# Attention sums of a graph network: one-hot matrices made on ScalarE, all weight products on VectorE, rings of eight

## The reference, cut to what matters

```
a = jnp.exp(a - amax[edge_dst])
a = a / (jax.ops.segment_sum(a, edge_dst, num_segments=n)[edge_dst] + 1e-12)
ns = jax.ops.segment_sum(vs * a[..., None], edge_dst, num_segments=n)...
nv = jax.ops.segment_sum(vv * a[..., None, None], edge_dst, num_segments=n)...
```

## Time and profile before

| | |
|---|---|
| runs | 12,377.51 us median (12,340.81 to 12,393.03) |
| span of the profiled execution | 13,633.7 us |
| first run of `attention_sums` | 3,190 to 3,757 us of the span |
| second run | 10,572 to 11,134 us |
| busy over the span | PE 70%, DVE 63%, POOL 59%, ACT 32% |

### The profile page before, as it was taken

How to read it: one execution, slowest core, us unless ns; L and a number is a source line. 1 busy time by engine, 2 the same in 40 slices (tenths; PEclk the granted TensorE clock), 3 DMA queues, 4 the chain that set the end, 5 groups by cost and what they waited for, 6 DMA issues and landing times. The chain is left out here.

```text
span 13633.7 us, 220854 instructions
## 1 busy us (share of the span) xinstructions
PE 9563.9 (70%) x44805; PEld 7451.6 (55%) x44805; DVE 8593.3 (63%) x21214; ACT 4334.4 (32%) x10856; POOL 8081.0 (59%) x8212
## 2 busy tenths in 40 slices
PE   2998989863656666666655777777775657888885
PEld 2888888853544222222244666666664545555554
DVE  4677777778734555555534777777777765555553
ACT  1444444430022222222212555555554002222221
POOL 4777777755624888888822555555552643555550
PEclk7777777777956777777765888888887987888885
DMA  3444444435602888888852222222221652222221
GB/s 93 105 107 103 107 102 107 105 100 158 188 20 50 132 132 132 131 132 131 132 148 85 68 69 68 68 69 69 68 69 49 183 134 57 71 71 70 73 72 46
DMA packets 1350634, 1320.06 MB, mean 97 GB/s; under 512 B 508622, under 2 KB 1147330, under 8 KB 1349894
## 3 DMA queue, kind: packets, MB, share of 16 engines
q0 software_dynamic: 347904, 594.12, 23.6%
q1 hardware_dynamic: 854716, 713.61, 18.2%
q10 hardware_dynamic: 147914, 11.21, 0.8%
HBM read 800.64 MB, written 517.55 MB: 97 GB/s over the span
## 5 line engine op out<-in xcount | busy, mean ns | idle before, releaser
L737 POOL DMA_INDIRECT e_gs<-tab_src,e_ix x1568 | 1685.9, 1075 | 1253.8 <-DVE e_msg L2066 785.5
L737 POOL DMA_INDIRECT e_gd<-tab_dst,e_ix x1568 | 1670.5, 1065 | 478.0 <-issue 473.4
L676 PE MATMUL e_psF<-w_ident,e_F 128*128 128x128 f32 x6272 | 1394.2, 335 | 727.6 <-ACT e_F L1954 495.6
L788 PE MATMUL e_psS<-e_rows,e_same 128*128 128x480 f32 x1568 | 1113.4, 876 | 857.7 <-DVE e_same L762 857.7
L1772 POOL DMA_INDIRECT e_g<-tab_src,e_er x976 | 977.0, 1001 | 852.0 <-DMA e_er<-edge_rows 600.8
L676 PEld LDWEIGHTS e_psF<-w_ident,e_F 128*128 128x128 f32 x6272 | 951.5, 180 | 895.9 <-issue 844.5
L806 POOL DMA_INDIRECT acc<-e_sums,e_row x784 | 1248.6, 1593 | 239.0 <-issue 220.5
L706 ACT ACTIVATE e_FT<-e_psF 128x384 f32<-128x384 f32 (+1 forms) x2352 | 1069.7, 455 | 941.7 <-PE e_psF L676 587.3
L788 PEld LDWEIGHTS e_psS<-e_rows,e_same 128*128 128x128 f32 x1568 | 431.4, 293 | 1549.4 <-issue 1522.2
L1563 PE MATMUL s_psS<-s_wv,s_hot 128*128 128x168 f32 (+1 forms) x3904 | 714.2, 331 | 596.0 <-POOL s_wv L1521 574.8
L712 ACT ACTIVATE e_O<-e_psO 128x352 f32<-128x352 f32 (+1 forms) x1568 | 689.7, 440 | 995.6 <-remote 434.0
(11 more groups left out here) (492 smaller groups left out, 25450.2 us busy)
## 6 DMA issues: line engine op xcount, KB each, us to landing
s_val<-val SPq DMA_DIRECT2D x488, 320.0 KB
val<-e_O SPq DMA_DIRECT2D x392, 320.0 KB
acc<-w_zeros SPq DMA_DIRECT2D x392, 139.5 KB
n_ag<-acc SPq DMA_DIRECT2D x56, 960.0 KB
e_krow<-in_src_t SPq DMA_DIRECT2D x196, 256.0 KB
sums<-e_total SPq DMA_DIRECT2D x244, 192.0 KB
e_es<-in_es SPq DMA_DIRECT2D x196, 130.0 KB
e_gs<-tab_src,e_ix POOLq DMA_INDIRECT x1568
```

The costliest lines, as they stand in the source:

```text
L676: last = nc.tensor.transpose(psF[:, P * g:P * g + P], F[:, k, P * g:P * g + P], ident[:, :])
L737: pool.indirect_dma_start(into[t][u][:, k, :], None, tables[t], bass.IndirectOffsetOnAxis(ix[u][:, t, k:k + 1], 0))\
L788: nc.tensor.matmul(psS[(k) % len(psS)], T["same"][u][:, k, :], values[:, k, :], start=True, stop=True)\
```

## The change

POOL keeps the shift, now in place in `key`, and copies the result into a float tile `rel` (a new instruction, with a wait between them), two steps behind the load; it also keeps the copy of the weights. ACT makes the one-hot matrices: four `Abs` activations of 128 columns each, |lane - rel|, with `rel` as per-partition bias, three steps behind the load, and one `Relu` of 1 - x over all 512 columns, a step later. DVE takes all weight products, one of 256 columns and three of 128. `val`, `pb`, `key` and `total` become rings of eight, the other buffers stay at four; the two semaphores `weighted_s` and `weighted_v` become `weighted` (DVE) and `copied` (POOL), and `key` gets a semaphore of its own. SP waits for one of them only. The hardware loop now holds eight steps.

```diff
-        RING = 4
+        RING, HALF = 8, 4
...
-        SUM, TOTAL, STORE, LAST = 1, 3, 7, 7
+        REL, APART, HOT, WEIGH, SUM, TOTAL, STORE, LAST = 2, 3, 4, 4, 5, 7, 10, 10
...
         def _(sp):
...
                 if m := i_of(0):
                     i, u, j = m
-                    wait_apart(sp, sem("weighted_s"), i - RING + 1, sem("sp_passed"))
-                    wait_apart(sp, sem("weighted_v"), i - RING + 1, sem("sp_passed"))
+                    wait_apart(sp, sem("weighted"), i - RING + 1, sem("sp_passed"))
...
         def _(pool):
...
-                    tt(rel[u][:, :], key[u][:, :], W["shift"][:, bass.ds(i, 1)].to_broadcast([P, TM]), ALU.add).then_inc(sem("rel"), 1)
-                    wait_apart(pool, sem("summed"), i - RING + 1, sem("pool_passed"))
-                    for d in range(2):
-                        weigh(tt, u, C0 + C1 * d, C1)
+                if m := i_of(REL):
+                    i, u, j = m
+                    wait_apart(pool, sem(f"key{u}"), (j + 1) * 16, sem("pool_passed"))
+                    wait_apart(pool, sem("apart"), i - HALF + 1, sem("pool_passed"))
+                    nc.gpsimd.tensor_tensor(key[u][:, :], key[u][:, :], W["shift"][:, bass.ds(i, 1)].to_broadcast([P, TM]), ALU.add)\
+                        .then_inc(sem("shifted"), 1)
+                    wait_apart(pool, sem("shifted"), i + 1, sem("pool_passed"))
+                    nc.gpsimd.tensor_copy(rel[u % HALF][:, :], key[u][:, :]).then_inc(sem("rel"), 1)
+                if m := i_of(WEIGH):
+                    i, u, j = m
+                    wait_apart(pool, sem(f"in{u}"), (j + 1) * 32, sem("pool_passed"))
+                    wait_apart(pool, sem("summed"), i - HALF + 1, sem("pool_passed"))
+                    nc.gpsimd.tensor_copy(wv[u % HALF][:, :, CX:width], pb[u][:, :, :]).then_inc(sem("copied"), 1)
...
         def _(dve):
...
-                    weigh(tt, u, 0, C0)
-                    weigh(tt, u, C0 + 2 * C1, C1).then_inc(sem("weighted_s"), 1)
-                    dve.wait_ge(sem("rel"), i + 1)
-                    tt(hot[u][:, :, :], bcast(W["lane"][:, :], 1, TM), bcast(rel[u][:, :], 2, P), ALU.is_equal).then_inc(sem("hot"), 1)
+                    tt(scalars(wv[u % HALF]), scalars(val[u]), bcast(pb[u][:, :, :], 3, C0 // H), ALU.mult)
+                    for d in range(3):
+                        part = lambda t: t[:, :, C0 + C1 * d:C0 + C1 * d + C1].rearrange("p t (h c) -> p t h c", h=H)
+                        last = tt(part(wv[u % HALF]), part(val[u]), bcast(pb[u][:, :, :], 3, C1 // H), ALU.mult)
+                    last.then_inc(sem("weighted"), 1)
...
         def _(act):
...
+                if m := i_of(APART):
+                    i, u, j = m
+                    act.wait_ge(sem("rel"), i + 1)
+                    wait(act, sem("summed"), i - HALF + 1)
+                    for k in range(TM):
+                        last = nc.scalar.activation(hot[u % HALF][:, k, :], W["lane"][:, :], ACT.Abs, bias=rel[u % HALF][:, k:k + 1], scale=-1.0)
+                    last.then_inc(sem("apart"), 1)
+                if m := i_of(HOT):
+                    i, u, j = m
+                    act.wait_ge(sem("apart"), i + 1)
+                    nc.scalar.activation(hot[u % HALF][:, :, :], hot[u % HALF][:, :, :], ACT.Relu, bias=1.0, scale=-1.0).then_inc(sem("hot"), 1)
```

More of the change, by code:

```diff
@@ L1472, in attention_sums @@
         ring = lambda name, shape, n, dt=F32: [S.sb(f"{name}{u}", shape, dt) for u in range(n)]
-        RING = 4
+        RING, HALF = 8, 4
         val, pb, key = ring("val", [P, TM, CX], RING), ring("pb", [P, TM, H], RING), ring("key", [P, TM], RING, I32)
-        rel, hot, wv = ring("rel", [P, TM], RING, I32), ring("hot", [P, TM, P], RING), ring("wv", [P, TM, width], RING)
+        rel, hot, wv = ring("rel", [P, TM], HALF), ring("hot", [P, TM, P], HALF), ring("wv", [P, TM, width], HALF)
         total = ring("total", [P, width], RING)
-        psS = [S.ps(f"psS{u}", [P, 512]) for u in range(RING)]
+        psS = [S.ps(f"psS{u}", [P, 512]) for u in range(HALF)]
         values, weights = blocks_of(D["val"]), blocks_of(D["probs"][H])
         targets = D["dst_sorted"].rearrange("p t -> (p t)").rearrange("(m q k) -> m q k", q=P, k=TM)
-        SUM, TOTAL, STORE, LAST = 1, 3, 7, 7
+        REL, APART, HOT, WEIGH, SUM, TOTAL, STORE, LAST = 2, 3, 4, 4, 5, 7, 10, 10
         block = ctx.enter_context(nc.Block())
-        def weigh(tt, u, a, n):
-            heads = lambda t: t[u][:, :, a:a + n].rearrange("p t (h c) -> p t h c", h=H)
-            return tt(heads(wv), heads(val), bcast(pb[u][:, :, :], 3, n // H), ALU.mult)
         @block.sync
@@ L1505, in _ @@
             for u in range(RING):
[L1506 removed]
+                sp.wait_ge(sem(f"stored{u}"), 16 * -(-(V - u) // RING))
         @block.gpsimd
         def _(pool):
[L1510 removed]
             def body(i_of):
[L1513 removed]
+                if m := i_of(REL):
                     i, u, j = m
[L1515 to L1521 removed]
+                    wait_apart(pool, sem(f"key{u}"), (j + 1) * 16, sem("pool_passed"))
[9 more added lines that the diff above has]
+                    nc.gpsimd.tensor_copy(wv[u % HALF][:, :, CX:width], pb[u][:, :, :]).then_inc(sem("copied"), 1)
             steps(pool, V, LAST, body, RING)
@@ L1530, in body @@
             def body(i_of):
-                if m := i_of(0):
+                if m := i_of(WEIGH):
                     i, u, j = m
-                    dve.wait_ge(sem(f"in{u}"), (j + 1) * 48)
-                    wait(dve, sem("summed"), i - RING + 1)
-                    weigh(tt, u, 0, C0)
-                    weigh(tt, u, C0 + 2 * C1, C1).then_inc(sem("weighted_s"), 1)
-                    dve.wait_ge(sem("rel"), i + 1)
-                    tt(hot[u][:, :, :], bcast(W["lane"][:, :], 1, TM), bcast(rel[u][:, :], 2, P), ALU.is_equal).then_inc(sem("hot"), 1)
+                    dve.wait_ge(sem(f"in{u}"), (j + 1) * 32)
+                    wait(dve, sem("summed"), i - HALF + 1)
+                    scalars = lambda t: t[:, :, 0:C0].rearrange("p t (h c) -> p t h c", h=H)
+                    tt(scalars(wv[u % HALF]), scalars(val[u]), bcast(pb[u][:, :, :], 3, C0 // H), ALU.mult)
[3 more added lines that the diff above has]
+                    last.then_inc(sem("weighted"), 1)
                 if m := i_of(TOTAL):
@@ L1545, in body @@
                     nc.vector.scalar_tensor_tensor(out=total[u][:, :], in0=total[(u - 1) % RING][:, :], scalar=W["keep"][:, bass.ds(i, 1)],
-                                                   in1=psS[u][:, 0:width], op0=ALU.mult, op1=ALU.add).then_inc(sem("totals"), 1)
+                                                   in1=psS[u % HALF][:, 0:width], op0=ALU.mult, op1=ALU.add).then_inc(sem("totals"), 1)
             dve.wait_ge(sem("empty"), 1)
@@ L1557, in body @@
                     i, u, j = m
-                    wait_apart(pe, sem("weighted_v"), i + 1, passed)
+                    wait_apart(pe, sem("copied"), i + 1, passed)
                     wait_apart(pe, sem("hot"), i + 1, passed)
-                    wait_apart(pe, sem("weighted_s"), i + 1, passed)
-                    wait_apart(pe, sem("totals"), i - RING + 1, passed)
+                    wait_apart(pe, sem("weighted"), i + 1, passed)
+                    wait_apart(pe, sem("totals"), i - HALF + 1, passed)
                     for k in range(TM):
-                        last = nc.tensor.matmul(psS[u][:, 0:width], hot[u][:, k, :], wv[u][:, k, :], start=(k == 0), stop=(k == TM - 1))
+                        last = nc.tensor.matmul(psS[u % HALF][:, 0:width], hot[u % HALF][:, k, :], wv[u % HALF][:, k, :],
+                                                start=(k == 0), stop=(k == TM - 1))
                     last.then_inc(sem("summed"), 1)
```

12 lines of the change are left out of this document (3 added, 9 removed).

## The result

Nineteen runs of the changed kernel have a median of 12,392.61 us (12,360.45 to 12,430.79), nineteen of the kernel before, beside them, 12,362.84 us (12,326.02 to 12,393.03). The ratio is 1.0028, 95% interval [1.0018, 1.0038]: slower by 0.28%, 30 us by the medians and 35 by the ratio. That is less than the 0.5% up to which the prediction spoke of no change, but nineteen runs of each tell it from zero, and the forecast was 10 us to the other side. One run of `rings_only` (19,271 us) and one of `cut_after` (21,517 us), both kernels of the experiments, fell into a slow state and are left out of the ratios.

What follows compares the result with a forecast made beforehand. SP's queue was taken as the bound, ACT's queue afterwards: 488 x 0.09 + 8 = +52 us in the profiled execution, turned into about -10 us for the runs, 12,365 us; range 12,250 to 12,600.

Steps and rivals of the forecast that it cites:

- The bound: Attention-sums function: SP's queue never stops and fills the step of 2.31 us; no engine or load bandwidth does.
- Deeper rings for nothing: Loads in the function: slots of the four-deep rings were already free, so deeper rings and earlier loads gain nothing.
- DVE, POOL and ACT's engine: Engine work per step: DVE 1.99 to 1.69 us, POOL 1.7 at most, ACT 1.8; none becomes the bound.
- ACT's queue becomes the bound: ACT's queue in the function: 2.0 + 0.43 - 0.04 = 2.39 us a step, 0.09 us above before.
- Fill and drain: Ends of each function run: three steps deeper, 4 us a run, 8 us in all.
- From the profile to the runs: Runs 9.2% below the span: perhaps stretched queue instructions; between a 20 us gain and 52 loss, about -10 us.
- +52: Sum in the profiled execution: 488 x 0.09 + 8 us on 13,633.7 us, +0.4%.
- Nothing outside these stretches is edited, so only what changes in a step counts: Stages outside the attention-sums function: no effect counted; only the time of its 488 steps was priced.
- A: Rival, faster: in real runs DVE, not the queues, bounds the function; step 1.85 us, gain 98 us, 12,280 us; chance 0.24.
- B: Rival, slower: ACT's queue costs more, at 0.8 us added a step of 2.75 us, 220 us, 12,600 us; chance 0.15.
- C: Rival, much slower: ACT's register reads or DMA issues wait for its empty engine; 3.8 us a step, 13,110 us; chance 0.08.
- D: Rival: `Abs` and `Relu` lie in different tables, two table loads a step, +1,252 us; chance 0.03.

Runs made afterwards that it cites:

- rings_only: Kernel before with the deeper rings, longer loop and earlier loads alone, work split as before: 12,362.6 us, 1.0003 of the kernel before.
- cut_after: Changed kernel with the last convolution left out and zeros in place of its sums, at low clock: 11,904.71 us, 0.8674 of the kernel before.
- split_only: Changed kernel with rings and loop of four again, the moved work alone: 12,361.52 us, 1.0014 of the kernel before.
- paired: Changed kernel with SP storing the totals of two steps by one DMA: 12,361.29 us, 0.9985 of the kernel before.
- fewer: Changed kernel with ACT's three ring waits before its loads left out: 12,377.99 us, 0.9998 of the kernel before.
- paired_rings: Kernel before with the deeper rings and earlier loads, plus totals of two steps stored by one DMA: 12,283.47 us, 0.9916 of the kernel before.
- before_again: Kernel before, unedited, profiled a second time: span 12,375.8 us, one run of 12,377.55 us.
- after_shifted: Changed kernel with eight repeated, long-met waits in SP's part of the function, in both calls: 12,322.05 us, 0.9973 of the kernel before.
- after_more: Changed kernel, unedited, run again beside the kernels with repeated waits: 12,377.12 us, 1.0018 of the kernel before.
- relieved_again: Changed kernel with paired stores of totals and without ACT's three ring waits, run a second time: 12,256.32 us, 0.9898 of the kernel before.

## Why the prediction was wrong where it was, and right where it was

**The bound (right).** SP's queue bound the function: with rings of eight, which alone gave nothing, and its stores paired, it fell from 560 to 501 us, while POOL was busy for 416 of these. Neither the engines nor the loads had been it.

**Deeper rings for nothing (right for the kernel before, wrong for the changed one).** `rings_only` is 1.0003. The prediction added that the cover would matter if the queues were quicker, and put it at nothing; `split_only`, where the moved work runs on rings of four, shows no gain (567 and 562 us), where with rings of eight it has 547 and 550: 20 and 12 us that hang on the deeper rings, the longer loop and the earlier loads together.

**DVE, POOL and ACT's engine (right, and without weight).** DVE 168.7 + 102.5 + 94.9 = 366 us in 244 steps, 1.50 us instead of the 1.69 I put (the products overlap), POOL's three instructions 60.7 + 51.3 + 55.7 = 168 us, 0.69 a step (0.66), ACT 438 / 244 = 1.80 us (1.8), its four activations 1.28 us (1.24 to 1.37). The three rows not yet shown:

```profile
L1533 DVE TENSOR_TENSOR s_wv<-s_val,s_pb 128x256 f32<-128x256 f32 x244 | 102.5, 420 | 9.6 <-DMA s_pb<-probs 6.5
L1544 DVE SCALAR_TENSOR_TENSOR s_total<-s_total,w_keep,s_psS 128x168 f32<-128x168 f32 x244 | 94.9, 389 | 209.3 <-PE s_psS L1562 208.1 <-issue 1.2
L1513 POOL CAST s_rel<-s_key 128x4 f32<-128x4 int32 x244 | 51.3, 210 | 38.8 <-POOL s_key L1510 37.5
```

The price of the Trainium skill, "ScalarE: Activation LUTs", "What ACT_TABLE_LOAD costs", 280 + 0.833 x 128 = an estimated 387 ns, is the 390 ns of the row. By its rules for kernel authors the relu belongs on VectorE; with it on ScalarE the function became 26 us shorter here, and ScalarE was busy for 1.80 of 2.23 us a step.

**ACT's queue becomes the bound (right), at 2.39 us (too high).** That it is the bound is shown by `paired` (SP relieved: nothing) against `fewer` (ACT relieved: 36 us). The step, and with it the distance of ACT's `key` issues, foreseen at 2.3 to 2.5 us, was 2.23 us. ACT's register reads, before and after in the same stretch:

```profile
L1576 ACTq TENSOR_LOAD <-w_block x131: 274/290/607, 3101.8 to 3399.9; - x131
```
```profile
L1576 ACTq TENSOR_LOAD <-w_block x135: 273/278/592, 3100.6 to 3399.3; - x135
```

Their mean, over all in the stretch, fell from 365 to 288 ns, and SP's from 413 to 315: why they are shorter isn't shown. And the trace has 1,864 records of ACT and its queue in 131 steps before, 2,729 in 135 after: 14.2 and 20.2 a step, five of the six new ones activations, where I had priced three to five register operations and waits beside them. If ACT's queue took 2.0 us before, the added work was 2.23 - 2.0 + 0.04 = 0.27 us a step, not 0.43. (That 2.0 us was never measured; in `paired_rings`, where this queue does the old work, the step is 501 / 244 = 2.05 us, so it was no more.) (Fill and drain, 8 us in my sum, can't be told from the noise: both functions are some 4 or 5 us longer than 243 of their steps.) The function was forecast 52 us longer and is 26 us shorter; 0.16 us a step too many make 78 us in 488 steps, the whole difference. SP's queue was sized too high as well: `fewer` was to be stopped by it at 2.19 us a step, 534 to 538 us, and it was, but at 2.12 us and 511.

**"From the profile to the runs" (the step that failed).** I took the 9.2% between span and runs for stretched queue instructions and so turned +52 into about -10. The function isn't stretched: it takes 561 to 563 us at either clock, and the spans of `before_again` and of the changed kernel are within 2 us of their run times. What differs are two other stages above all, the layer 2 edges and the last convolution, here in the first trace of the kernel before and then in `before_again` (columns as in the earlier trace rows):

```profile
7413.50:10454.10 3040.60, 2240.22 (x13296) 2037.11 (x13296) 2220.86 (x4887) 1594.10 (x4885) 1727.86 (x1568) 0.83 0.26 68
11387.70:13288.30 1900.60, 1588.44 (x6100) 999.03 (x6100) 1082.89 (x2441) 519.65 (x1465) 1038.57 (x1220) 0.83 0.26 72
```
```profile
7236.40:9521.80 2285.40, 1920.51 (x13296) 1751.68 (x13296) 2191.79 (x4886) 1537.99 (x4885) 1736.25 (x1568) 0.94 0.35 90
10460.60:12029.10 1568.50, 1453.74 (x6100) 942.28 (x6100) 1086.43 (x2441) 509.36 (x1465) 1031.12 (x1220) 0.92 0.32 87
```

They are 755 and 332 us of the 1,258 between the two spans. The lower clock goes with them, but it doesn't account for all: length times clock of the last convolution is 1,577 us in the first trace and 1,443 in the second, and PE is busy for 84% of it there and 93% here. What else differs between such executions is open. A sign of all this was there: the span's granted clock, 0.770, beside a span that no run had. The function, whose bound is a queue, should have been carried over unchanged. That would have given +52, nearer to the +30 or 35 of the runs, but for the wrong reason: a function that gained 26 and a loss of 56 to 61 elsewhere.

**"Nothing outside these stretches is edited, so only what changes in a step counts" (the other step that failed).** It is true of the instructions and not of what they cost. The prediction put the effect of the change on the other stages at nothing; it was a loss of 56 to 61 us. Of that, four more instructions in each call of SP's program give back all (`after_shifted`: function -25, whole -33), and in `fewer` nearly all. Shown is that the loss isn't one of the moved work: it goes with the length of SP's program ahead of the stage. That the place of the later code is what counts is argued from this; how it reaches TensorE's clock is open. The 131 ns gap goes with the loss, the jump doesn't. POOL waits longer for `edge_rows` in `after_more` than in `after_shifted`, but nearly as long, 280.8 and 273.6 us, in `paired` and `relieved_again`, which have neither gap. Waits in the last convolution, `after_more` and `after_shifted`:

```profile
POOL e_g L1783 <- DMA e_er<-edge_rows: 284.3, 134, 16.9
```
```profile
POOL e_g L1784 <- DMA e_er<-edge_rows: 221.4, 117, 16.9
```

**The rivals.** A: false; the function took 561 us in a trace as fast as the runs. B: false; the step is 2.23 us, not 2.75. C: false by the timeline of 3300.09 to 3302.17. D: false; no table load stands in the function.

**What the change is worth by itself.** With the four instructions added, 0.9973 [0.9965, 0.9982], about 33 us faster. Of that the deeper rings and the moved work have their part only together. The fastest kernel, `relieved_again`, is 126 us ahead of the kernel before, and `paired_rings`, which moves no work, already 104: its function takes 501 and 510 us against 492 and 494, 25 us more, and it still has ACT's three waits, so the moved work itself is worth at most that.

## What to carry to other kernels

When no engine fills a loop's step, count the step of each queue, register reads and waits with it, and relieve the fullest; moving engine work onto an engine with the second fullest queue mostly changes which queue it is. Before carrying a profile over to the runs, set its span and its granted clock beside them: if they differ, each stage differs by its own bound, not all by one factor. When a change gains in its own function and not in the whole, compare the untouched stages, and run the kernel once with a few idle instructions added to the program before them: a loss that this takes away doesn't come from the work that was changed. If nothing happens, that clears nothing: three kernels here stayed as they were.

## What the runs showed of the hardware

The kernel before takes 12,350 us at a mean granted clock of TensorE of 0.80, or 13,720 us at 0.77. The chip had the number 3 in runs of both kinds, so it isn't a matter of the chip alone. A queue-bound function took the same 561 to 563 us in both.

From the branch of a hardware loop on SP's queue to the next instruction it takes 102 to 128 ns in some loops and 195 to 248 ns in others, steady within a loop at the upper clock; two loops of one kernel can differ (123 ns in the second run of the function and in the last convolution of `after_shifted`, 219 in the first run of the function). In the last convolution the dear jump costs nothing, since a wait follows it.

Four instructions more in each of two calls of SP's program, which only found a semaphore long met, changed a kernel by 55 us, another by 94; in both, a stage in which PE is 92% busy kept the upper clock more often, and a gap of 131 ns in SP's queue was back at 51. In three other kernels such instructions changed nothing.

A register read from SBUF by a queue takes 263 ns at best on SP's and 273 on ACT's, and in the kernel before up to 697 on SP's (390 in the median). ACT's queue goes on while its engine computes: it read a register and began to issue a load within four activations of 1.28 us.
